# A selective scan in eight passes: two images in one direction against one image in two directions, with its rows fetched from device memory

## The reference, cut to what matters

```
xs = concat([x, x_transposed, flip(x), flip(x_transposed)])      # K = 4 directions, DI = 96 channels, L = 256 tokens
dt, B, C = split(xs @ x_proj);  dt = softplus(dt @ dt_proj + bias)
for each token t:                                                # N = 16 states per channel
    h = h * exp(dt[t] * A) + (dt[t] * u[t]) * B[t]
    y[t] = sum over the 16 states of h * C[t]
out = y summed over the four directions in their own order, + D * x
```

## Time and profile before

| what | us |
|---|---|
| median of 3 runs | 463.25 (460.02 to 463.73) |
| the profiled execution | 463.01 |
| its span (first to last instruction) | 461.3 |
| first scan starts, last scan ends | 41.0, 311.0 |
| busy: PE, DVE, POOL, ACT | 371.3, 346.4, 206.9, 179.8 |

### The profile page before, as it was taken

How to read it: one execution, slowest core, us unless ns; L and a number is a source line. 1 busy time by engine, 2 the same in 40 slices (tenths; PEclk the granted TensorE clock), 3 DMA queues, 4 the chain that set the end, 5 groups by cost and what they waited for, 6 DMA issues and landing times. The chain is left out here.

```text
span 461.3 us, 5553 instructions
## 1 busy us (share of the span) xinstructions
PE 371.3 (80%) x1669; PEld 214.3 (46%) x1669; DVE 346.4 (75%) x622; ACT 179.8 (39%) x405; POOL 206.9 (45%) x210
## 2 busy tenths in 40 slices
PE   5825499697887867857999998896989999969691
PEld 4612133142332312323557555553865786958450
DVE  5885989878999999999789898987457356263514
ACT  2565354554563534423243332335225211135340
POOL 7131697867895967774653863451121010000001
PEclk9999889979897987785999999999799989588966
DMA  5502212011121110110101010000000000000000
GB/s 121 106 21 64 56 26 64 23 41 34 23 58 34 47 40 18 40 43 9 47 21 33 11 34 1 0 2 1 2 17 1 1 0 17 2 1 1 1 17 18
DMA packets 15743, 12.69 MB, mean 28 GB/s; under 512 B 7279, under 2 KB 11361, under 8 KB 15713
## 3 DMA queue, kind: packets, MB, share of 16 engines
q1 hardware_dynamic: 15713, 12.33, 11.7%
HBM read 2.62 MB, written 0.79 MB: 7 GB/s over the span
## 5 line engine op out<-in xcount | busy, mean ns | idle before, releaser
L559 POOL TENSOR_TENSOR outp<-state,c_rep 128x512 f32<-128x512 f32 x96 | 126.4, 1321 | 93.0 <-PE y_acc L1397 43.1
L1019 DVE TENSOR_TENSOR_SCAN state<-decay,inp_bc 128x512 f32<-128x512 f32 x96 | 117.2, 1221 | 9.3 <-DVE inp_bc L1010 4.3
L1397 PE MATMUL y_acc<-outp,band 128*96 128x512 f32 x192 | 111.2, 666 | 6.7 <-DVE y_sum L1034 2.6
L732 ACT ACTIVATE decay<-step_bc,a_neg 128x510 f32<-128x510 f32 x96 | 64.9, 683 | 47.0 <-PE step_bc L1384 46.8
L1010 DVE TENSOR_TENSOR inp_bc<-b_rep,inp_bc 128x512 f32<-128x512 f32 x96 | 65.5, 682 | 7.1 <-PE inp_bc L1388 6.9
L1388 PE MATMUL inp_bc<-room_s,spread 96*128 96x512 bf16 x96 | 41.0, 427 | 31.1 <-DVE state L1019 31.0
L494 POOL TENSOR_TENSOR rs<-mv,neg_half 128x2 f32<-128x2 f32 x16 | 11.1, 696 | 120.0 <-DVE mv L1055 119.9
L1384 PE MATMUL step_bc<-room_s,spread 96*128 96x512 bf16 x96 | 39.9, 415 | 12.7 <-DMA room_s<-lo 11.6
L1397 PEld LDWEIGHTS y_acc<-outp,band 128*96 128x96 f32 x192 | 34.3, 182 | 24.7 <-issue 10.3
L1388 PEld LDWEIGHTS inp_bc<-room_s,spread 96*128 96x128 bf16 x96 | 9.9, 103 | 65.9 <-DVE state L1019 56.8
L1384 PEld LDWEIGHTS step_bc<-room_s,spread 96*128 96x128 bf16 x96 | 10.4, 109 | 32.5 <-issue 27.3
(11 more groups left out here) (346 smaller groups left out, 650.8 us busy)
## 6 DMA issues: line engine op xcount, KB each, us to landing
b_rep<-bc SPq DMA_DIRECT2D x64, 32.0 KB, 1.9
c_rep<-bc SPq DMA_DIRECT2D x64, 32.0 KB, 2.0
room_s<-hi SPq DMA_DIRECT2D x24, 64.0 KB, 2.0
room_s<-mid SPq DMA_DIRECT2D x24, 64.0 KB, 2.0
room_s<-lo SPq DMA_DIRECT2D x24, 64.0 KB, 2.0
x_tok<-in_x_dram SPq DMA_DIRECT2D x2, 384.0 KB, 3.8
out_dram<-room_g SPq DMA_DIRECT2D x4, 192.0 KB, 2.0
room_a<-in_L_attn_w_qkv_dram SPq DMA_DIRECT2D x1, 432.0 KB, 6.5
```

The lines of the kernel that those rows point to most:

```text
L559: g.tensor_tensor(outp[:, u % SLOTS, :], state[:, u % STATE_SLOTS, :], c_rep[:, n % 2, :], ALU.mult).then_inc(S["outp"], 1)
L732: a.activation(decay[:, u % SLOTS, :, 1:L], step_bc[u % 2][:, :].rearrange("p (b l) -> p b l", b=IMG)[:, :, 1:L], ACT.Exp, scale=a_neg[:, ...
L1019: v.tensor_tensor_scan(state[:, u % STATE_SLOTS, :], decay[:, u % SLOTS, :, :].rearrange("p b l -> p (b l)"), inp_bc[u % 2][:, :], 0.0, AL ...
L1397: t_.matmul(y_acc[0:DI, :], band[:, at:at + DI], outp[:, u % SLOTS, :], start=(g12 == 0), stop=(g12 == UNITS - 1)).then_inc(S["y_mm"], 1)
```

## The change

**A pass is one image in two directions.** Passes 2i and 2i+1 belong to image i: forwards (rows, columns) and backwards. Nothing is copied backwards any more: the backward pass scans the same data with reversed access patterns, and `decay` is zero at the other end. A unit is 16 channels x 8 states instead of 8 x 16; a pass is 6 groups of channels for each half of the states, so there are still 12 units a pass and 96 in all. `y_acc` collects the two passes of an image; `add_y` comes once per image.

**The rows come from device memory.** `spread_out`, the three-part split and the stack are gone. The step sizes and inputs of a pass are written to a device memory tensor (384 KB), and each unit reads 16 rows of 4 KB, each onto 8 partitions (512 KB), into one of four `in_rep` slots, issued from SP. C goes the same way (two transfers of 256 KB a pass). B times the input still needs B on 128 partitions: PE makes it directly with repeated weights (`fill_b`, two products of 256 columns for each half of the states) in two PSUM banks. `decay` comes from SBUF by two exponentials of 255 columns with a scale each, and has two slots per direction; `drive` writes one PSUM bank, `drv`, so it waits for the scan before.

**The sums over the states** write 32 rows each; units are ordered so that three in a row belong to the three thirds of the 96 rows, and their products are issued together (`BATCH`), four units behind, with six `outp` slots.

**The planner** lets image n start after unit 24(n+1)+4: 68 of 132 steps (33 per image, the two halves of the weighing being one step) stand beside units: all 33 of image 0, 27 of image 1, 8 of image 2. 64 follow. The front computes one image's convolution on DVE; the others' are on PE beside units.

```
-RING = 3
-SLOTS = 3
+RING = 4
+SLOTS = 6
+IN_SLOTS = 4
+DECAY_SLOTS = 2
-Y_LAG = 3
+BATCH = CHUNKS
+Y_LAG = 4
-PRE_HI, PRE_REST, PRE_MID, PRE_LO = (2, 3), (4, 5), (5, 6), (6, 6)
+FILL_B = (-4, 2)
+AT_ROWS, AT_STEP, AT_REPEAT = 0, 3, (7, 13)
...
+def unit(u):
+    n, g = u // UNITS, u % UNITS
+    third, q = g % GROUPS % CHUNKS, g % GROUPS // CHUNKS
+    return n // PER_IMAGE, n % PER_IMAGE, g // GROUPS, PER_CHUNK * third + q
...
+def keep_step(n):                                               # SP
+    sp.wait_ge(S["step"], n + 1)
+    if n >= 2:
+        sp.wait_ge(S["decay"], UNITS * (n - 1))
+    sp.dma_start(step_rows[n % 2], step2[0:DI, :, :]...).then_inc(S["step_kept"], 16)
+def repeat_step(u):
+    if u % UNITS == 0:
+        sp.wait_ge(S["step_kept"], 16 * (n + 1))
+    if u >= IN_SLOTS:
+        sp.wait_ge(S["decay"], u - IN_SLOTS + 1)
+        sp.wait_ge(S["drive"], u - IN_SLOTS + 1)
+    rows = step_rows[n % 2, GRP * g:GRP * (g + 1), :]
+    sp.dma_start(in_rep[:, u % IN_SLOTS, :, :]..., rows.unsqueeze(1).to_broadcast([GRP, SN, 2 * TOK]))
...
+def expo(u):                                                    # ACT
+    act.wait_ge(S["in_there"][slot], 16 * (u // IN_SLOTS + 1))
+    if u >= DECAY_SLOTS:
+        act.wait_ge(S["state"], u - DECAY_SLOTS + 1)
+    for e in range(WAYS):
+        ins = a.activation(decay[:, back, u % DECAY_SLOTS, e, kept], in_rep[:, slot, 0, :]...[:, e, kept],
+                           ACT.Exp, scale=a_neg[:, at:at + 1])
...
+def drive_of(u):                                                # DVE
+    if u:
+        dve.wait_ge(S["state"], u)
+    v.tensor_tensor(drv[:, :], in_rep[:, slot, 1, :], b_bc[part][:, :], ALU.mult).then_inc(S["drive"], 1)
+def scan(u):
+    v.tensor_tensor_scan(state[...][:, order], held[:, order], drv[:, :][:, order], 0.0, ALU.mult, ALU.add)
...
+def fill_b(n, part):                                            # PE
+    for e in range(WAYS):
+        ins = t_.matmul(b_bc[part][:, e * L:(e + 1) * L], w_b[:, k, part, :], xs[:, i, e, :], start=True, stop=True)
+def sum_states(first):
+    pe.wait_ge(S["outp"], first + BATCH)
+    for u in range(first, first + BATCH):
+        rows = slice(CHUNK * (c16 // PER_CHUNK), CHUNK * (c16 // PER_CHUNK + 1))
+        t_.matmul(y_acc[rows, :], band[:, at:at + CHUNK], outp[:, u % SLOTS, :], ...)
```

More of the change, by code:

```diff
@@ L120, in side_work @@
             ready[n] = u + UNITS_AFTER.get(step, UNITS_AFTER_ELSE)
-    at = {step: i for i, step in enumerate(steps)}
-    done += [0, 0]
     rest = []
@@ new lines, in _ @@
+            keep_c(0)
+            keep_step(0)
+            for u in range(2):
+                repeat_step(u)
+            for i in range(PARTS):
+                repeat_c(0, i)
+            for u in range(2, IN_SLOTS):
+                repeat_step(u)
+            for u in range(SLOT_COUNT):
+                n, at = u // UNITS + 1, u % UNITS
+                later = SECOND_LATER if n == 1 else 0
+                if n < SCANS and at == AT_ROWS + later:
+                    keep_c(n)
+                if n < SCANS and at == AT_STEP + later:
+                    keep_step(n)
+                if n < SCANS and at == AT_REPEAT[0]:
+                    repeat_c(n, 0)
+                if n > 1 and at == AT_REPEAT[1] - UNITS:
+                    repeat_c(n - 1, 1)
+                if u + IN_SLOTS < SLOT_COUNT:
+                    repeat_step(u + IN_SLOTS)
@@ L676, in weights @@
+            for n in range(1, IMAGES):
+                group_normed(n)
+            for n in range(1, IMAGES):
+                pad(n)
             def weights(step):
@@ L712, in pre_softplus @@
                 a.activation(spl[:], spe[:], ACT.Ln, bias=1.0).then_inc(S["sp_ln"], 1)
-            def pre_hi(n, i):
-                act.wait_ge(S["step"] if i else S["sp_max"], n + 1)
-                if n > 0:
-                    for j in range(CHUNKS):
-                        act.wait_ge(S["stack"][j], 16 * 3 * n)
-                a.copy(hi[:, i, :], step2[:, i, :]).then_inc(S["hi"], 1)
-            def pre_mid(n, i):
-                act.wait_ge(S["rest"], 2 * n + i + 1)
-                a.copy(mid[:, i, :], step2[:, i, :]).then_inc(S["mid"], 1)
@@ L913, in _ @@
+            group_bias(0, one)
+            turned_stats(2, 1)
+            for c in range(2):
+                turned_stats(3, c)
+            collected(1, IMAGES, 2 * IMAGES)
             for e in range(2):
@@ L1290, in _ @@
             done(ins)
-            group_means(0)
+            turn_input(2)
+            group_vars(0, one)
+            turn_input(3)
             b_ = begin("w_xp")
@@ new lines, in pre @@
+            def pre(n):
+                b_ = begin(f"d{n}")
+                for e in range(WAYS):
+                    ins = way(b_, n, e)
+                done(ins)
+            def fill_b(n, part):
+                if n:
+                    pe.wait_ge(S["drive"], UNITS * (n - 1) + GROUPS * (part + 1))
+                i = n // PER_IMAGE
+                pe.wait_ge(S["xs"], i + 1)
+                for e in range(WAYS):
+                    k = WAYS * (n % PER_IMAGE) + e
+                    ins = t_.matmul(b_bc[part][:, e * L:(e + 1) * L], w_b[:, k, part, :], xs[:, i, e, :], start=True, stop=True)
+                ins.then_inc(S["b_there"], 1)
@@ L1595, in side @@
                     done(ins)
-            front("z", 0)
+            for n in range(1, IMAGES):
+                inner(n)
             b_ = begin("d0")
```

846 lines of the change are left out of this document (379 added, 467 removed).

## The result

The changed kernel takes **481.55 us** (median of 4 runs, 476.67 to 482.76), the kernel before 462.47 on the same chip (460.02 to 463.73): a ratio of 1.04, 95% interval 1.0311 to 1.0488. It is slower by 19 us; 449 had been forecast, with a range that ended at 476.

The account below looks back on a forecast made before the run. DVE was taken to bound the scans with PE close behind, PE and a chain the stretch behind them. Front 40 + scans 286 + tail 121 = 447, plus 1.7 around it: 449 us, range 440 to 462.

Parts of the forecast that it names:

- The tail, "121 us": Stretch behind the last scan: 112.8 us from the old trace plus drain, small steps and a lone end; 121 against 150.3.
- The sign given for a wrong forecast: Behind the last scan: a tail staying over 130 us because the ends of images 2 and 3 are chains, not PE's work.
- The scans, "286 us": The 96 units: 177.6 + 4 + 27 + 49.4 + 7 + 21 = 286 us, 16 more than before.
- idle 21: DVE's idle time in the scans: 21 us instead of 26, from decay stalls, transfers, first clip, gates, PE and order.
- DVE idle over 35 us, ended by decay: Sign in the scans that the forecast is wrong: DVE idle over 35 us, with decay ending the waits.
- More steps beside the scans is the heart of it: DVE's step work within the scans rises to 49.4 us from 29, as images 0 to 2 do more steps there.
- Off the path: PE.: PE in the scans: spreading dropped, three sums become one set; PE did not set the scans, so only DVE's idle gains.
- The front, "40": Stretch before the first scan: it starts at 40 us against 41, bounds 38 and 44.
- bias at 25.6: In the front: first bias at 25.6 us instead of 27.60, with the other images' normalisation ahead of it on ACT.
- the rival of the two decay slots: In the scans: each of 68 steps costs 0.55 us, not 8 of them: 477 us; if half, 463; chance 0.13.
- Transfers: Row reads on SP's queue: 2.3 us a unit, under 3.0; rival has 3.2 setting the pace, 473 us, chance 0.13.
- the remainder, 31 us: DVE's scan time in the old trace beside scan, drive and preparation: about 9.5 us of y sums, gates, weights, and 45 steps.

## Why the prediction was wrong

**The tail, "121 us", is the step that failed**: it is 136.0. Its term of 112.8 us was taken from the trace of before, for the stretch behind the first turned probabilities of image 1; from the same state the changed kernel takes 481.0 - 349.3 = 131.7. The forecast gave that stretch no term for the score stage, which weighs once behind `t1` in place of twice, although the list of the change has it ("the two halves of the weighing being one step"), and none for TensorE's clock, 0.76 in it for 0.83. On the planner of before, putting the two halves and their banks back took 12 us off the run, part of it by way of the clock.

In the changed kernel itself the split wasn't tried, and its rows point to two places. Between the output products of images 2 and 3 it takes 27.0 us, before 19.9: there the last weighing stands. Between those of images 1 and 2 it takes 77.7 us, before 61.9: one weighing stands there too, but the longest waits of DVE are the 20.0 us for `at`, before 4.3, with one step of the other image between `cx` and `at`, and the products of `at` at half clock (5.2 to 5.3 us for the 24). How the 15 us divide among weighing, `at` and clock stays open. The sign given for a wrong forecast, a tail over 130 us because the ends of images 2 and 3 are chains, did come.

**The scans, "286 us"**, are 300. The floor with the wait for `drv` was put at 1.97 us and is 2.05, since that wait costs 0.2 and not 0.12: some 3 us over the 35 empty units that the forecast counted. DVE's own work was rather over-estimated: 258.6 us busy for 265. The term that failed is "idle 21": it is 41.5, and 15.2 of it are the four waits at `cx` and `at`, one unit apart, with products on a clock of 1.2 GHz. Spacing them gave the forecast's 285, so this part is found; that it would not shorten the run, since five steps came back behind the scans at 2.6 us each, was not seen. The sign "DVE idle over 35 us, ended by decay" came by half: decay ends 11.2 of the 41.5, 8.2 of them at `cx`.

**"More steps beside the scans is the heart of it"**: no. With the planner wholly undone the run is 485.0 against 481.6, ranges overlapping (476.2 to 486.5, 476.7 to 482.8). The forecast had 20 more us of steps in the scans against 29 less behind them; measured are 29 less in the scans and 30 more behind them when they are moved back.

**"Off the path: PE."** Half right: DVE is the busiest engine in the scans, and keeping PE busy with other work brought nothing. But the forecast never mentioned the granted clock, which fell from 0.90 to 0.68, and batched sums were priced at zero; undoing them moved the median by 3.3 us in the changed kernel and 8.8 on the planner of before, each time with ranges that overlap. Whether that is a gain, and by clock or by earlier sums, is not settled.

**The front, "40"**, is 44.9. The term "bias at 25.6" counted ACT's six normalisations and forgot the twelve input products that the same three images put on TensorE, 4.92 us. Moved away, the bias came at 26.02 and the scan at 40.73.

**Right:** the backward scan at no price (1220 to 1223 ns in all 96). Value steps wait 0.61 us (0.55 forecast), a pair of exponentials takes 0.91 (0.84); the rival of the two decay slots gave 477, near the result, for a reason that isn't the result's. Transfers: a median of 4.9 us from issue to landing for 512 KB, hidden, as the run without them shows. Between 44 and 108 us the share is 0.97 at 242 GB/s, so the 603 kB of a unit take 2.5 us (2.3 forecast). The fit of the Trainium skill (DMA: Bandwidth & Descriptors, Anatomy of one DMA), measured on POOL's queue, gives an estimate of 2.0 + 524/436 = 3.2 us for such a read; the trace, with SP's queue, has 4.9 and decides.

**Two readings of the trace of before were off**, with little effect on the forecast. "At most 266 GB/s" is not so: from 2 to 5 us the same trace has 314 at a share of 1.01. And "the remainder, 31 us" takes the sum of single groups from a total in which overlaps count once; the ledger behind it, with 29 of steps and 9.5 of others, is the one that closes.

## What to carry to other kernels

Price every edit of the diff, the merged step too: what must stand behind the last operation of a chain costs its whole length there. Splitting a reduction so that its first half runs under the next stage, with its banks, was worth 12 us of 476 here. Moving side work under a loop that is 86% busy on its bound engine saves behind the loop about what it costs in it (22 against 27 us, 15 against 13, 29 against 30). Take a low granted clock as something to explain. Three times it was raised with added products, and three times the run gained nothing over their price; but the same steps took 149.9 us at 0.87 and 159.1 at 0.79. And look at the clocks of two executions before putting the difference of their profiles down to an edit.

## What was not expected of the hardware

A scan on DVE with one operand in PSUM took 1.22 us each of 96 times, whatever POOL did; with both in SBUF it did so all 28 times that POOL stood still, and took up to 2.36 us beside POOL's products (in the rows above it ends 1.08 us after the second of them, so it ran behind it). The Trainium skill (SBUF — State Buffer, Who interferes with whom) says that a DVE instruction with two SBUF inputs contends with a GpSimd instruction that reads SBUF; these rows agree.

TensorE's clock can stand at 1.2 GHz while its records lie back to back: 13.00 of 13 us busy at 0.55 in the stretch above. In that run, the one without the split, it fell behind the 24 products of 34 columns of `cx`: the same eight query products took 1.90 us at 366.20, ahead of them, and 3.70 at 371.18, behind them. Such a group of 24 takes 2.77 us at full clock (`at` of image 2 in the run with the split) and 5.33 at half. Executions of one kernel differ in it too: with a mean clock of 0.867 the run with the split weighing took 461.4 us, with 0.842 it took 471.4, and its three longest executions of ten are those under 0.85. That time and clock go together is shown, which of them leads is not.
